# A graph layer and a sparse expert layer in one launch: where the expert weights are staged, and when they are loaded and converted

## The reference

```
# graph layer
h   = layernorm(x)
agg = segment_sum(h[src], dst);  deg = segment_sum(1, dst)
x1  = x + h @ W_self + (agg / max(deg, 1)) @ W_neigh + b
# expert layer: 16 experts, the two best for each node
t      = layernorm(x1)
logits = t @ gate_w + gate_b;  the 2 largest, softmax over the 2
h_e    = relu(t @ w1[e] + b1[e])      # w1[e]: 256 x 512
y_e    = h_e @ w2[e] + b2[e]          # w2[e]: 512 x 256
out    = x1 + layernorm(t + sum of the two weighted y_e) * gamma + beta
```

## Time and profile before

| | |
|---|---|
| median of 3 runs | 781.57 us |
| the profiled execution: its time | 781.5 us |
| its span in the trace | 779.5 us |
| TensorE busy | 571.9 us, 73% |
| VectorE busy | 502.7 us, 64% |
| ScalarE busy | 365.8 us, 47% |
| mean granted clock of TensorE | 0.883 of full speed |
| ScalarE, line 836 (high halves) | 60 times, 37.6 us busy, 133.5 us idle before it, ended by a load |
| VectorE, line 1331 (low halves) | 60 times, 41.4 us busy, 86.9 us idle before it |

### The profile page before, as it was taken

One profiled execution on the slowest core, in us unless ns is written; L12 is line 12 of the kernel. 1 busy time (PEld: TensorE's weight loads), 2 busy tenths in 40 slices (PEclk: granted clock), 3 DMA queues, 4 the chain that ended last, 5 costly groups with the idle time before them and its releaser, 6 DMA issues.

```text
span 779.5 us, 14732 instructions
## 1 busy us (share of the span) xinstructions
PE 571.9 (73%) x5135; PEld 459.7 (59%) x5135; DVE 502.7 (64%) x1422; ACT 365.8 (47%) x894; POOL 284.7 (37%) x456
## 2 busy tenths in 40 slices
PE   1869877676777677766678773788888888888760
PEld 0435566555566555555557663677777777777650
DVE  4676666667667656766767779656555555565585
ACT  2436544333344333433334321567666666667522
POOL 4711022112132112221113210665666667554264
PEclk9989888788688878879869895899999999999995
DMA  9200121122212212112210020325222222223798
GB/s 217 56 1 1 28 68 55 55 74 75 67 54 61 68 55 88 54 55 74 79 36 18 24 63 32 105 70 148 70 70 76 76 68 68 69 53 77 178 196 125
DMA packets 41239, 56.69 MB, mean 73 GB/s; under 512 B 5347, under 2 KB 30171, under 8 KB 41166
## 3 DMA queue, kind: packets, MB, share of 16 engines
q1 hardware_dynamic: 30896, 36.73, 17.3%
q0 software_dynamic: 9440, 18.28, 9.3%
q10 hardware_dynamic: 830, 0.74, 0.4%
HBM read 39.73 MB, written 17.99 MB: 74 GB/s over the span
## 4 chain that ended last, share of the span: by engine, by line
PE 35%; DVE 19%; DMA 15%; ACT 10%; issue 7%; another core or an unknown queue 6%; POOL 4%; SPq 1%; DVEq 1%; ACTq 0%; POOLq 0%
DMA W<-in_L_ffn_w 11%; PE PS L1111 6%; PE PS L1027 6%; PE PS L1028 6%; PE PS L1015 5%; PE PS L1123 5%; PE PS L965 3%; ACT arena L881 2%; DVE W L1331 2%; ACT W L836 2%; DVE W L1315 2%; POOL arena L710 2%; DMA W<-z_tab 2%; DMA arena<-xh_tab,tok_of 1%
## 5 line engine op out<-in xcount | busy, mean ns | idle before, releaser
L1027 PE MATMUL PS<-arena,AGG 125*128 125x257 f16 x625 | 182.4, 319 | 0.1
L1028 PE MATMUL PS<-arena,AGG 125*128 125x256 f16 x625 | 179.6, 314 | 0.0
L804 ACT ACTIVATE AGG<-PS 128x500 f16<-128x500 f32 (+1 forms) x175 | 91.4, 540 | 89.2 <-PE PS L1015 88.9
L1111 PE MATMUL PS<-arena,AGG 128*128 128x128 f16 x1536 | 102.8, 221 | 23.0 <-DVE AGG L1504 13.7
L1015 PE MATMUL PS<-W 128*128 128x125 f16 x416 | 76.2, 291 | 56.8 <-DVE W L1315 56.4
L1111 PEld LDWEIGHTS PS<-arena,AGG 128*128 128x128 f16 x1536 | 89.2, 98 | 30.5 <-DVE AGG L1504 16.9
L1123 PE MATMUL PS<-AGG,arena 128*128 128x256 f16 x768 | 98.2, 273 | 6.0 <-issue 5.7
L836 ACT ACTIVATE W<-W 128x512 f16<-128x512 f32 x60 | 37.6, 627 | 133.5 <-DMA W<-in_L_ffn_w 133.5
L692 POOL DMA_INDIRECT z_tab<-arena,meta_of x64 | 74.6, 1166 | 70.1 <-ACT arena L897 55.7
L701 POOL TENSOR_SCALAR arena<-arena 125x1 f32<-125x1 f32 x23 | 8.0, 349 | 251.6 <-DVE arena L1346 251.6
L1517 DVE TENSOR_TENSOR arena<-arena 128x512 f16<-128x512 f32 x64 | 44.1, 691 | 84.4 <-ACT arena L890 83.2
(11 more groups left out here) (243 smaller groups left out, 946.4 us busy)
## 6 DMA issues: line engine op xcount, KB each, us to landing
W<-in_L_ffn_w SPq DMA_DIRECT2D x60, 256.0 KB
xh_tab<-arena SPq DMA_DIRECT2D x25, 125.0 KB
out<-arena SPq DMA_DIRECT2D x24, 125.0 KB
W<-z_tab SPq DMA_DIRECT2D x2, 1344.0 KB
W<-z_tab SPq DMA_DIRECT2D x2, 896.0 KB
W<-in_x SPq DMA_DIRECT2D x2, 672.0 KB
AGG<-out SPq DMA_DIRECT2D x2, 672.0 KB
out<-W POOLq DMA_DIRECT2D x2, 672.0 KB, 6.9
```

Source lines behind the costliest of these rows:

```text
L804: a.activation(AT[j % 2][:, :, QT * GD * s:QT * GD * s + n * GD].rearrange("p h (g l) -> p h g l", l=GD), p_A[(BQ * j + s) % 4][:, 0:n * B ...
L1027: t.matmul(p_agg[j % 2], AT[j % 2][0:BT, h, :], HW[0:BT, h, D:HS - 1], start=(h == 0), stop=False)
L1028: ins = t.matmul(p_agg[j % 2][:, 0:D], AT[j % 2][0:BT, h, :], HW[0:BT, h, 0:D], start=False, stop=(h == NB - 1))
L1111: ins = t.matmul(p_h[s % 2][:, c * P:(c + 1) * P], w1e[:, s % 2, wa, k, c * P:(c + 1) * P], xT[:, s % 2, xa, k, :], start=(y == 0), stop=( ...
```

## The change

Staging. The two staging places are replaced: piece n is staged in the final place of piece n+4 (`stage_of`). High and low half of a piece are one float32 piece in size together, so it fits. The last pieces have no such place, and use the room of the last expert of `W2`, as before. The load's target is now in two runs of 1 KB in each partition for every piece, also for those of `w1`, where it was one run of 2 KB.

Waits. Load n waits for the high half of piece n-4 instead of the low half of piece n-2 (the last four also for the low half of piece n-2), so that up to four loads are under way. There are four load semaphores instead of two. ScalarE's high half n also waits for the low half of piece n-4, since that one is read from the place that it writes.

Order. The first four loads wait for the end of the prologue (`loop_open`), because `X` and the prologue's scratch lie in the places that they write. Conversions run in passes 1 to 19 with three pieces each, and passes 20 and 21 have one and two. The load issued at a slot is that of the piece four further on.

The fallback's `FBT` goes from 17 to 5, which gives back semaphores.

```diff
-FBT = 17
+FBT = 5
+STAGES = 4
...
-        stage = [w2_f[:, LASTW + v * PIECE:LASTW + (v + 1) * PIECE] for v in range(2)]
+        def piece_place(n):
+            e, c = divmod(n, 4)
+            w = W1 if c < 2 else W2
+            return w[:, e, :, :, :].rearrange("p a k f -> p a (k f)")[:, :, (c % 2) * PIECE:(c % 2 + 1) * PIECE]
+        def stage_of(n):
+            later = n + STAGES
+            if later >= NPIECE + 2:
+                later = NPIECE + n % 2
+            if later >= NPIECE:
+                later += 2
+            return piece_place(later).bitcast(f32)
...
         def slot_piece(i, r):
-            n = SLOTS * i + r
-            return n if n < NPIECE else None
+            if i < 1 or i > 21:
+                return None
+            if i == 20:
+                return NPIECE - 3 if r == 0 else None
+            if i == 21:
+                return NPIECE - 3 + r if r > 0 else None
+            return SLOTS * (i - 1) + r
...
             def weight_load(n):
-                if n is None:
+                if n is None or n >= NPIECE:
                     return
-                _, _, there, here = weight_piece(n)
-                if n >= 2:
+                _, _, _, there, here = weight_piece(n)
+                if n >= STAGES:
+                    sp.wait_ge(w_hi, n - STAGES + 1)
+                if n + STAGES >= NPIECE + 2:
                     sp.wait_ge(w_lo, n - 1)
-                sp.dma_start(here, there).then_inc(w_loaded[n % 2], DMA)
-            for i in range(NB):
-                weight_load(slot_piece(i, 0))
-                weight_load(slot_piece(i, 1))
-                if i >= 1:
-                    xx_store(i - 1)
-                weight_load(slot_piece(i, 2))
-                if i >= 1:
-                    xh_store(i - 1)
+                sp.dma_start(here, there).then_inc(w_loaded[n % STAGES], DMA)
+            def next_load(i, r):
+                n = STAGES + SLOTS * (i - 1) + r
+                if i == 21 and r < 2:
+                    return NPIECE - 2 + r
+                return n if n < NPIECE - 2 else None
+            sp.wait_ge(loop_open, 1)
+            for n in range(STAGES):
+                weight_load(n)
+            for i in range(1, NB):
+                weight_load(next_load(i, 0))
+                weight_load(next_load(i, 1))
+                xx_store(i - 1)
+                weight_load(next_load(i, 2))
+                xh_store(i - 1)
...
-                act.wait_ge(w_loaded[n % 2], DMA * (n // 2 + 1))
-                a.activation(hl[:, 0, :], stage[n % 2], ACT.Copy, scale=scale).then_inc(w_hi, 1)
+                act.wait_ge(w_loaded[n % STAGES], DMA * (n // STAGES + 1))
+                if n >= STAGES:
+                    act.wait_ge(w_lo, n - STAGES + 1)
+                a.activation(hi, stage, ACT.Copy, scale=scale).then_inc(w_hi, 1)
...
                 dve.wait_ge(w_hi, n + 1)
-                v.scalar_tensor_tensor(hl[:, 1, :], stage[n % 2], scale, hl[:, 0, :], ALU.mult, ALU.subtract).then_inc(w_lo, 1)
+                v.scalar_tensor_tensor(lo, stage, scale, hi, ALU.mult, ALU.subtract).then_inc(w_lo, 1)
```

More of the change, by code:

```diff
@@ L216, in build @@
         oh = [oh_extra] + [w1_f[:, LASTW + v * P * QT:LASTW + (v + 1) * P * QT].bitcast(f16).rearrange("p (h j u) -> p h j u", h=2, u=QT) for v in range(2)]
-        stage = [w2_f[:, LASTW + v * PIECE:LASTW + (v + 1) * PIECE] for v in range(2)]
+        def piece_place(n):
[9 more added lines that the diff above has]
+            return piece_place(later).bitcast(f32)
         def weight_piece(n):
             e, c = divmod(n, 4)
-            w, t, scale = (W1, w1, WS1) if c < 2 else (W2, w2, WS2)
-            hl = w[:, e, :, :, :].rearrange("p a k f -> p a (k f)")[:, :, (c % 2) * PIECE:(c % 2 + 1) * PIECE]
+            t, scale = (w1, WS1) if c < 2 else (w2, WS2)
             if c < 2:
-                there = t[e, c * P:(c + 1) * P, :]
-                here = stage[n % 2]
+                there = t[e, c * P:(c + 1) * P, :].rearrange("p (a f) -> p a f", a=2)
             else:
                 there = t[e, (c - 2) * 2 * P:(c - 1) * 2 * P, :].rearrange("(c p) d -> p c d", p=P)
-                here = stage[n % 2].rearrange("p (c d) -> p c d", d=D)
-            return hl, scale, there, here
+            place = piece_place(n)
+            hi, lo = [place[:, a, :].rearrange("p (c d) -> p c d", c=2) for a in range(2)]
+            return hi, lo, scale, there, stage_of(n)
         BK = NB * 2
@@ L375, in build @@
         agg_done = sem("agg_done")
-        w_loaded = [sem(f"w_loaded{v}") for v in range(2)]
+        w_loaded = [sem(f"w_loaded{v}") for v in range(STAGES)]
         w_hi = sem("w_hi")
@@ L833, in weight_high @@
                     return
-                hl, scale, _, _ = weight_piece(n)
-                act.wait_ge(w_loaded[n % 2], DMA * (n // 2 + 1))
-                a.activation(hl[:, 0, :], stage[n % 2], ACT.Copy, scale=scale).then_inc(w_hi, 1)
+                hi, _, scale, _, stage = weight_piece(n)
+                act.wait_ge(w_loaded[n % STAGES], DMA * (n // STAGES + 1))
+                if n >= STAGES:
+                    act.wait_ge(w_lo, n - STAGES + 1)
+                a.activation(hi, stage, ACT.Copy, scale=scale).then_inc(w_hi, 1)
             act.wait_ge(cleared, 3)
@@ L1328, in weight_low @@
                     return
-                hl, scale, _, _ = weight_piece(n)
+                hi, lo, scale, _, stage = weight_piece(n)
                 dve.wait_ge(w_hi, n + 1)
-                v.scalar_tensor_tensor(hl[:, 1, :], stage[n % 2], scale, hl[:, 0, :], ALU.mult, ALU.subtract).then_inc(w_lo, 1)
+                v.scalar_tensor_tensor(lo, stage, scale, hi, ALU.mult, ALU.subtract).then_inc(w_lo, 1)
             def x1_norm(j):
```

## The result

The changed kernel takes 742.34 us (median of 4 runs, 739.12 to 747.79) where the kernel before takes 782.91 us (median of 4 runs, 780.86 to 784.81). The ratio is 0.949, with a 95% interval of 0.942 to 0.956. The profiled execution took 743.68 us with a span of 741.9 us.

A forecast was written before the change was run, and what follows sets the result against it. Weight loads issued late behind stores in SP's list were taken to bound the loop. Gains of 26.9 + 5.9 + 2.6 + 0.3 less 2.1 added make 33.6 us: 781.5 to 747.9, say 748, range 740 to 756.

The forecast's parts named there:

- rival (c): Store of x1 late for VectorE's x1_norm, if it needs over 6 us; 766 us for one more; chance 0.05.
- The pass with six batches: Loop passes with six one-hot batches: 13.75 us, or 15.3 with TensorE's slow end, one in three; 14.25 taken.
- The pass with seven: One loop pass in four, with seven one-hot batches: from 18.36 us to 14.7 to 15.5, 15.0 taken.
- The pass after it: Pass behind one with seven batches, long at 1.2 GHz: 13.43 us without conversions plus 1.0, taken as 14.5.
- Slot 1: VectorE's low half of slot 1 waits 1.03 us because ScalarE's high half stands behind the third eviction; that stays.
- a tight load: Load 58, issued about 0.5 us before pass 21, used some 6 us into it: tight by 0 to 1 us.
- The signs of being wrong: VectorE waiting for stores in x1_norm, sixth batch later than 11.3 us into the pass, or loop clock under 0.75.
- (a): TensorE's clock in the loop falls further, or pass ends are slow: 756 to 766 us; chance 0.16.
- (b): Conversions hide better, all loop passes at the full clock: 730 to 740 us; chance 0.11.
- (d): No change, the loads' waits turn into equal waits elsewhere: 778 to 783 us; chance 0.04.
- (e): Slower, TensorE at 1.2 GHz through the whole loop: 791 us; chance 0.04.
- Left at nothing: ScalarE's new low-half wait, halves' times, tile strides, prologue and fallback jump, SP's stores: all taken as no cost or gain.

The follow-up runs named there:

- the extra products: The changed kernel with 12 extra products of 256 columns on TensorE ahead of the first and sixth quad of each pass; 736.06 us, ratio 0.936.
- the fastest version: The changed kernel with slot 1's high half behind the second eviction, sixth batch ahead of place_rows, seventh right behind place_rows; 702.75 us, ratio 0.894.

## Why the prediction was right, point by point

*Where the loads were late.* The prediction said that loads were late by their place in SP's list. The new order of the list alone gives 743.1 us, and four places with the old order give 782.0. Both were needed to show it, since the change moved places, waits and order together. The mechanism was right; its terms were off by 0.1 to 0.6 us a pass in passes 2 to 19 and by 1.5 in pass 20, in part against each other, as below.

*How long a load takes: this was misread.* I gave 4.8 to 5.9 us, median 5.3, for all the weights' loads from the earlier trace rows. The page's own table of DMA issues of the kernel before shows what that row holds:

```profile
W<-in_L_ffn_w SPq DMA_DIRECT2D x60, 256.0 KB
...
AGG<-in_L_ffn_w SPq DMA_DIRECT2D x1, 512.0 KB, 4.8
arena<-in_L_ffn_w SPq DMA_DIRECT2D x1, 512.0 KB, 5.9
```

The 60 loads have no landing time in it; the three numbers are the two loads of twice the size, for the last expert, and their mean. A load of 256 KB issued at 221.17 was followed by its high half at 224.59:

```profile
224.59 0.63 ACT L836 ACTIVATE W<-W 128x512 f16<-128x512 f32 x1 [3.67 <-DMA W<-in_L_ffn_w]
```

That is 3.4 us. The changed kernel's table has a landing time for these loads:

```profile
W<-in_L_ffn_w SPq DMA_DIRECT2D x60, 256.0 KB, 3.0
```

So the median is 3.0 us there, and 3.5 in the kernel with four places and late loads. The sum did not use the number, since the loads go out ahead of their use by more than either number (14 us at the least, 8.1 and 10.6 for the last two); but by it I expected the two places to fail at passes of 12 us, and they don't, and the condition of rival (c) was reckoned with a load of 5.9 us.

*The pass with six batches.* Forecast 13.75 us at the full clock and 15.3 with a slow end. Measured: 13.3 to 13.9 in six of nine, not counting those that follow a pass with seven batches, and 14.95, 15.05 and 15.77 in the others, mean 14.11 against 14.25. The ends compare directly, from the sixth batch to gate_out, in the changed kernel:

```profile
118.38:122.95 4.57, 3.79 (x20) 3.00 (x20) 1.62 (x4) 1.38 (x3) 0.00 (x0) 0.63 0.33 104
275.82:278.78 2.96, 2.22 (x20) 1.98 (x20) 1.62 (x4) 1.38 (x3) 0.00 (x0) 1.00 0.45 132
```

The terms were 4.50 us at 0.62 and 2.95 at 1.00: the same stretch has the same two prices in the new kernel. The sixth batch was put at 10.8 us into the pass and came at 10.4 to 10.8 in those six.

*The pass with seven.* Forecast 15.0, measured 14.34 to 15.87, mean 15.34. Its seventh batch was put at 12.4 us and came at 12.2 to 12.8; three of the five have the slow end. *The pass after it:* forecast 14.5, measured 13.42 to 14.36, mean 13.9. Here I took the long slow stretch of before (a clock of 0.72) as given. It is there behind two passes with a slow end (14.10 and 14.36 us, clock 0.72 and 0.73) and is not behind the two whose end was at the full clock (13.42 and 13.78 us, 0.87 and 0.88). That is 0.6 us a pass in the mean of the four. In pass 20 I forecast 0.3 us more and it took 1.2 less, at a clock of 0.81 instead of 0.72. Over passes 2 to 19 these errors cancel in part: 1.3 us too much for the nine passes, 1.7 too little for the five with seven batches, 2.3 too much for the four behind them. That the forecast for these passes, 32.8, came within 2.0 us of the measured 34.8 is luck to that extent.

*Slot 1.* Forecast: this wait is the third eviction and stays, 1 us or so each. It stayed, 26.4 us in 18 passes, so 1.5 each and up to 2.0, and the eviction moved behind the half removes it there. In pass 21, where I had named a tight load, VectorE waited 2.23 us, but the load had gone out at 377.99, 1.4 us before the pass began, and ScalarE's high half came at 386.13, right behind the third eviction: not the load.

*The signs of being wrong.* One came in one pass: the sixth batch of the pass from 138.82 starts 11.52 us in, later than the 11.3 named. It is a pass behind one with seven batches, at a mean clock of 0.73, so the sign was set too close and not the mechanism wrong. Before gate_out VectorE waits 1.2 to 1.5 us in 12 of the 18 passes, as named, and 2.4 to 3.0 in the other six, those with a slow end.

*The rivals.* (a) A lower clock: it rose, 0.87 over the loop against 0.81. (b) The full clock: 742 lies between it and the forecast, and the extra products show what it gives, 13.67 us a pass over 18 passes. The page "TensorE: Matmul & The Clock Gate" of the Trainium skill (section "What's actually happening") says that the throttle is the default and activity releases it; these products are the trace's case for it. (c) Late stores: no wait for a store in the loop. The ordering rule of the page "DMA: Bandwidth & Descriptors" of the Trainium skill (section "Queues, rings and completion order") was neither seen nor refuted here, because no store was needed soon enough. (d) and (e) did not come.

*Left at nothing.* One-KB runs instead of 2 KB: 3840 more packets, and queue q1's share of the span times the span is 134.9 us before (17.3% of 779.5) and 132.8 after (17.9% of 741.9), so nothing. The halves have medians of 0.62 and 0.68 us, before 0.63 and 0.69. ScalarE's new wait for a low half does not show among its waits.

## What to carry to other kernels

Where a load is late, look first at what stands ahead of it in its queue's list and what that waits for; a deeper ring of buffers costs memory and semaphores and may add nothing. After such a repair follow the path by the last wait in a pass, instruction by instruction: here gains of 39, 30 and 28 us lay in moving instructions past others that they did not depend on (the last two give 33 together). Price a stretch of TensorE at both clock levels, and say which waits will go, because the clock follows them.

## What the runs showed of the hardware

With TensorE's waits filled the clock was 1.00 for 251 us. With its waits for VectorE left in, up to 2.8 us long before and up to 2.1 after, it was 0.81 in the kernel before, 0.87 in the changed one, 0.90 with slot 1 earlier and 0.92 in the fastest version. Filling such waits with products that nobody reads paid where both waits were about 1.5 us or longer (1.4%, though by the times on two chips only 6 us) and cost 26 us where one of them was under 0.5. A load of 256 KB landed 3.0 us after its issue in the median, one of 512 KB after 4.8 and 5.9.
